# Two mixer load waits added, 25 idle matrix products removed, in a one-core MoE and state-space kernel

## The reference

```python
x = x + 0.5 * ffn(layernorm(x))      # 8 experts, each token in its best 2
x = x + mixer(layernorm(x))          # rms norm, projections, 3-tap conv, two scans, gate
x = x + 0.5 * ffn(layernorm(x))
# ffn: scores = softmax(x @ Wg); of the 2 best experts e:
#      silu(x @ W11[e]) * (x @ W12[e]) @ W2[e], weighted and summed
```

## Time and profile before

| | before |
|---|---|
| median of 3 runs (lowest to highest) | 958.73 us (958.6 to 959.55) |
| the profiled execution, its own time | 965.39 us |
| its span, first to last instruction | 963.6 us |
| PE busy | 904.5 us, 94% |
| DVE, ACT, POOL busy | 583.7, 389.3, 575.2 us |
| granted PE clock, mean | 0.983 of full speed |

### The profile page before, as it was taken

One profiled execution on the slowest core, in us unless ns is written; L12 is line 12 of the kernel. 1 busy time (PEld: TensorE's weight loads), 2 busy tenths in 40 slices (PEclk: granted clock), 3 DMA queues, 4 the chain that ended last, 5 costly groups with the idle time before them and its releaser, 6 DMA issues.

```text
span 963.6 us, 19180 instructions
## 1 busy us (share of the span) xinstructions
PE 904.5 (94%) x5458; PEld 773.9 (80%) x5459; DVE 583.7 (61%) x1386; ACT 389.3 (40%) x768; POOL 575.2 (60%) x616
## 2 busy tenths in 40 slices
PE   7979999999999999958999996999999999999994
PEld 7748888888888888845876873788888888888883
DVE  4876565665656655558836997555555555555551
ACT  3834343343343433315634775233333333333331
POOL 4845655665655666417604653477777777777762
PEclk9989999999999999989999998999999999999998
DMA  9743616436254373149202556744433434333331
GB/s 322 259 145 124 209 57 205 164 98 202 66 190 157 106 241 124 39 157 300 90 0 88 173 161 216 246 103 79 80 54 71 79 52 77 54 76 54 54 45 23
DMA packets 83745, 121.51 MB, mean 126 GB/s; under 512 B 12944, under 2 KB 62480, under 8 KB 83696
## 3 DMA queue, kind: packets, MB, share of 16 engines
q0 software_dynamic: 25088, 37.59, 17.8%
q1 hardware_dynamic: 43504, 56.05, 17.7%
q10 hardware_dynamic: 15104, 27.28, 8.5%
HBM read 73.62 MB, written 47.25 MB: 125 GB/s over the span
## 4 chain that ended last, share of the span: by engine, by line
PE 81%; DVE 6%; issue 4%; DMA 3%; ACT 2%; POOL 1%; another core or an unknown queue 1%; ACTq 1%; POOLq 0%; SPq 0%; DVEq 0%
PE bank L1501 37%; PE bank L1524 19%; PE bank L1510 6%; PE bank L1623 3%; PE bank L1684 3%; PE bank L1493 3%; PE bank L1436 3%; PE bank L1674 1%; PE bank L1703 1%; PE bank L1640 1%; DMA w_lo<-w_lo_rows 1%; DMA out_rows<-yb,idx_i 1%; PE bank L1611 1%; PE bank L1694 1%
## 5 line engine op out<-in xcount | busy, mean ns | idle before, releaser
L1204 DVE TENSOR_TENSOR sg<-sg,bank 128x512 f32<-128x512 f32 x142 | 97.6, 687 | 283.3 <-ACT sg L758 188.0
L1501 PE MATMUL bank<-w_hi,xt_hi 128*128 x568 | 237.3, 418 | 7.7 <-DVE xt_lo L1193 4.2
L1501 PE MATMUL bank<-w_hi,xt_lo 128*128 x568 | 224.1, 394 | 0.0
L1501 PE MATMUL bank<-w_lo,xt_hi 128*128 x568 | 223.9, 394 | 0.0
L750 ACT ACTIVATE yb<-bank,gates_in 128x256 f32<-128x256 f32 x142 | 67.3, 474 | 315.9 <-PE bank L1524 252.5
L554 POOL DMA_INDIRECT xg<-xn_rows,idx_i x142 | 139.9, 985 | 61.6 <-issue 42.0
L558 POOL DMA_INDIRECT gates_in<-gate_rows,idx_g x142 | 135.8, 957 | 53.7 <-issue 42.7
L1524 PE MATMUL bank<-w_hi,ft_hi 128*128 x568 | 160.1, 282 | 2.2 <-ACT yb L750 2.2
L1524 PE MATMUL bank<-w_lo,ft_hi 128*128 x568 | 160.3, 282 | 0.0
L1524 PE MATMUL bank<-w_hi,ft_lo 128*128 x568 | 160.2, 282 | 0.0
L568 POOL DMA_INDIRECT out_rows<-yb,idx_i x71 | 114.7, 1616 | 59.0 <-ACT yb L750 27.5
(11 more groups left out here) (290 smaller groups left out, 1297.8 us busy)
## 6 DMA issues: line engine op xcount, KB each, us to landing
w_lo<-w_lo_rows SPq DMA_DIRECT2D x32, 512.0 KB
w_lo_rows<-w_lo ACTq DMA_DIRECT2D x16, 512.0 KB
xn_rows<-work SPq DMA_DIRECT2D x13, 512.0 KB, 3.2
x_all<-x SPq DMA_DIRECT2D x8, 512.0 KB, 10.3
w_lo_rows<-in_sb ACTq DMA_DIRECT2D x16, 256.0 KB
gate<-x SPq DMA_DIRECT2D x16, 256.0 KB, 7.8
seq<-y_rows SPq DMA_DIRECT2D x8, 512.0 KB, 5.2
seq<-w ACTq DMA_DIRECT2D x7, 512.0 KB
```

The source lines that it names most:

```text
L1204: nc.vector.tensor_tensor(sg[p], sg[p], ps_g[p][:], ALU.mult).then_inc(f_step, 1)
L1501: last = nc.tensor.matmul(dst[p][:], xt[p][:, c, :], of(w), start=(c == 0 and n == 0), stop=(c == DC - 1 and n == len(parts) - 1))
```

## The change

Two things change. In the mixer's first pass, SP and ACT issue the blocks of chunk 1 only after both blocks of chunk 0 have landed (`y_in` of its buffer at 32). In both routers, the idle products in front of groups 2 and 3 are left out: 10 + 7 in the first, 8 in the second.

```diff
             for p in range(2):
                 sp.wait_ge(y_out[p], 16 * ((ET + 1 - p) // 2))
             load_y(0)
+            sp.wait_ge(y_in[y_buffer[0]], 32)
             load_y(1)
             sp.wait_ge(m_ready, 1)
             load_y(2)
...
             for i in range(2):
+                if i == 1:
+                    act.wait_ge(y_in[y_buffer[0]], 32)
                 act.dma_start(y_place[y_buffer[i]][1].rearrange("p (j d) -> p j d", d=D),
...
                 for n in range(NQB):
-                    if n >= 2:
-                        idle = ((10, 7), (8, 0))[r][n - 2]
-                        keep_busy(ps_g[0][:], before.unsqueeze(1).to_broadcast([P, G, P]), idle)
                     pe.wait_ge(first_step, r * NQB + n + 1)
                     pe.wait_ge(by_p_ready, r * NQB + n + 1)
```

## The result

The change made the kernel slower. Seven runs of it have a median of 964.14 us (961.83 to 965.43), seven of the kernel before beside them 959.19 us; the ratio is 1.0039, with a 95% interval of 1.0027 to 1.0050. That is +3.7 us (2.6 to 4.8) where +0.8 was forecast, and 964.1 lies outside the range of 957.3 to 961.0. The profiled execution of the change took 961.83 us (span 960.1), the shortest of its seven, so its trace shows the loss at its smallest.

The account below looks back on a forecast made before the run. PE, busy nearly all the time, was taken as the bound, so only its standstills or half clock count. Mixer +0.2, first router 0, second +0.6 gave +0.8 on 958.73: 959.5 us, range 957.3 to 961.0.

Parts of the forecast that it names:

- The mixer's term: Mixer's start, two added waits: +0.3 for late chunk 1, -0.2 for chunk 0 landing sooner, +0.1 for chunk 3; +0.2 us.
- The 0.1 for chunk 3: Mixer: chunk 3 would land at 444.0, DVE's cover for it just used up; 0.1 us added.
- The estimate of 4.4 us: Mixer: landing time of chunk 0's 1 MB, from a fixed 2.0 us plus bytes at 436 GB/s.
- 0.8 of the 1.1 is thus hidden, and 0.3 shows: Mixer: DVE gets chunk 1 1.1 us late; ACT took up its norm 0.8 after POOL's last step, so 0.3 us remains.
- Behind chunk 1 on SP stand chunk 2, four input blocks, and later chunk 3: Mixer, SP's queue: the wait opens a DMA gap of 2 to 2.5 us, so chunk 3 would land at 444.0.
- a gain that is given back: Mixer: PE's first transposes gain at most about 1.3 us, but chunk 1's norm has no such gain.
- The slower rival through the mixer's loads: Mixer: chunk 1 shares engines with chunk 2, takes 8.2 us and costs +2.9; 962.2 with the router's +0.6; chance 0.06.
- The first router: 17 idle products out: group 3 at half clock, first tiles perhaps at full clock; 0 us, bounds -1.2 and +0.7.
- The second router: 8 idle products out: group 2 starts 0.5 sooner but the clock may stay low; +0.6 us, bounds -0.2 and +1.8.
- rise midway: Second router: the clock rises midway through the late groups 2 and 3, held likeliest; about +0.7 us.
- the case priced at +1.2: Second router: clock low for both groups 2 and 3, which take 3.9 us from 590.4 until 594.3; +1.2 us.
- The sum of the routers: Both routers, idle products out: 0 for the first and +0.6 us for the second.

## Why the prediction was wrong

**The mixer's term, +0.2 with bounds -0.7 and +1.2: wrong.** It measured +2.2 us in the change's own trace and +3.3 with the waits alone, by time +4.1 (2.9 to 5.4). The landings were right: chunk 0 at 5.29 us from issue, chunk 1's sum 0.9 late (forecast 1.1), POOL's steps of chunk 0 short, chunk 1's transposes not late. In the earlier trace rows chunk 0 took 5.58, so the gain was 0.3 (forecast 0.2). The 0.1 for chunk 3 was nothing: no engine waited for its load. The estimate of 4.4 us that the forecast drew from the Trainium skill ("DMA: Bandwidth & Descriptors", Anatomy of one DMA) is not borne out: chunk 0 travelled without chunk 1 here and took 5.29.

The step that failed is "0.8 of the 1.1 is thus hidden, and 0.3 shows", together with "Behind chunk 1 on SP stand chunk 2, four input blocks, and later chunk 3". It followed only chunk 1's own norm, where indeed nothing was lost. It missed two things.

1. *The other consumers of DVE's time.* Behind chunk 1's sum, DVE has the add of chunk 2, which needs the buffer that chunk 0's store empties, and then `rows_low(0)`, which PE's first gate products need. The store had no room to spare: in the kernel before it was issued at T+8.24 and landed 7.7 us later, 0.2 before the add. In the change it stands on SP behind all those loads, was issued at T+9.52 and landed 8.6 later. DVE, 0.9 late from chunk 1's sum, reached the add at 434.73 - 1.85 = T+16.33, near the T+16.17 of before, and stood until T+18.18, 2.0 later than before. From there the delay goes straight on to `rows_low(0)` and to PE's gate products, which wait 1.38 us for it, start 1.6 late, and cost the mixer 1.4 (83.5 against 82.1, in both runs with the store late and full clock). With the store late and chunk 1 in time (SP's wait alone) the add was 0.5 to 1.0 late and the mixer 0 to 0.3 longer. With chunk 1 late, the store moved and full clock, the mixer was still 1.2 longer (83.29), since POOL's step beside the add of chunk 2 then makes chunk 1's transposes 1.0 late. So moving the store gave back 0.2 of the 1.4. What the loss can't do without is chunk 1's 0.9, and two ways lead from it to PE, of which the forecast had neither; it had put the cover for DVE at chunk 3, one step further on.

2. *PE's clock.* PE's first transposes came 1.8 us sooner (forecast: at most 1.3) and chunk 1's no sooner, so PE stood still longer, 3.14 instead of 1.40 us, and again before the gate products. The clock then fell to half (0.50 at 440 to 442), where before it was full. That cost 0.8 us in the change's trace (84.26 less 83.47) and 1.8 with the waits alone (85.36 less 83.52). The forecast named the clock at both routers and not here; sooner transposes were booked as a gain that is given back, not as a gap.

The runs with idle products show the second by taking it away. For the first there are the chain and the runs with one half missing; no run took it away cleanly. With the store moved, POOL's longer step takes the store's place, so the two can't be added up.

**The slower rival through the mixer's loads (962.2)** came closer in time, but not in its mechanism: chunk 1 took no 8.2 us in the change. Only ACT's wait alone brings that about, with 8.12.

**The first router, 0 with bounds -1.2 and +0.7: within its bounds, -0.8 by the mean of the traces; by time -1.1 in one pair of kernels and 0 in another.** Group 3 went to half clock (2.05 us, forecast 1.96). The forecast compared with a tile 0 at half clock, from the one trace it had; 8 of the 12 profiles with the 17 products have it at full clock. Tile 0 was 0.3 later than in that trace (forecast 0.6) and 0.2 earlier in the mean. The shorter gap ahead of tile 0, which the forecast named and did not price, is part of the gain.

**The second router, +0.6 with bounds -0.2 and +1.8: direction right, too small, +1.6 in the mean and +1.1 in the change's own trace (17.4 us to tile 0, against 16.3).** In the change the clock did not "rise midway": both late groups ran at half clock, 3.95 us, just the case priced at +1.2. Group 2 began 0.4 sooner, as said. In the kernel with all 25 removed the groups were at full clock and tile 0 paid instead, so which of them pays is not fixed.

**The sum of the routers** was forecast +0.6 and is +0.8 by the traces and +0.7 (-0.2 to +1.5) by time. That it comes out so near is in part luck: the forecast was too low for the second router and too high for the first. Nearly the whole miss is the mixer's. Waits and idle products alone add up to 4.1 + 0.7 = 4.8 us, at the upper end of the change's 2.6 to 4.8.

What stays open: with the same gaps of PE (0.34 and 1.36, 0.33 and 1.39 us) the clock stayed full in one kernel and fell in another, and how long it stays low differs between the change and the waits alone. Each of these gaps is from one execution. The runs show what the fall costs, not what decides it.

## What to carry to other kernels

Before a wait is put into a DMA queue, list every issue behind it until the queue is level again, stores as well as loads, and follow for each store who waits for its buffer; the data that is delayed on purpose is only one of the delays, and a transfer with 0.2 us to spare, as the store had, becomes a wait. Do the same for the compute engine that uses the held-back data: list what it does next, and who waits for each of these steps. Then look at what TensorE does with the change: an earlier piece of work followed by an equally late one is a longer gap, and here such a gap cost another 0.8 to 1.8 us in half clock. A load held back until another has landed should be held back on all the queues that carry it, or not at all: with ACT's half waiting while SP went on to six later loads, that half landed 8.12 us after its issue and DVE stood still 3.73 us. Held back on SP alone it cost nothing here, and gained nothing.

## What the runs showed of the hardware

Three things were not expected. A block of 512 KB issued on ACT's queue 1.4 us after SP had begun to issue six others took 8.12 us to land, against 5.32 for the first. Thirteen more products whose results nobody reads made the kernel with the waits some 2.6 us faster, although the gate products started no sooner (T+22.82, without them T+22.73). And idle products that held the clock when placed right ahead of a late group (15.6 to 16.6 us to tile 0) did less, by the traces, when they stood ahead of the whole router (16.8 and 17.5; without them 17.4 to 18.2).
